# Dot attention on one Trainium2 core: one-hots built ahead of the sums over features, queries gathered one group ahead

## The reference, cut to what matters

```python
def _L2_gnn_ref(embeds, qW, kW, vW, rows, cols):      # rows = src, cols = dst
    q = (embeds[rows] @ qW).reshape(e, HEADS, dh)     # HEADS = 4, dh = 24
    k = (embeds[cols] @ kW).reshape(e, HEADS, dh)
    v = (embeds[cols] @ vW).reshape(e, HEADS, dh)
    scores = jnp.clip(jnp.einsum('ehd,ehd->eh', q, k), -10.0, 10.0)
    exp_s = jnp.exp(scores)
    norms = jax.ops.segment_sum(exp_s, rows, num_segments=nvar)[rows]
    w = exp_s / (norms + 1e-08)
    res = jax.ops.segment_sum(w[:, :, None] * v, rows, num_segments=nvar).reshape(nvar, d)
    return embeds + res
```

## Time and profile before

| | |
|---|---|
| median of 3 runs | 1662.23 us (1661.86 to 1662.38) |
| profiled execution | 1663.21 us, of which the span of the trace is 1661.0 us |
| mean granted clock of TensorE | 0.888 |
| busy over the span | PE 1248.2 us (75%), DVE 1260.6 us (76%), ACT 551.0 us (33%), POOL 379.8 us (23%) |
| dot attention, groups | from 1244.1 us (first one-hot) to 1564.8 us (last addition) |

### The profile page before, as it was taken

One profiled execution on the slowest core, in us unless ns is written; L12 is line 12 of the kernel. 1 busy time (PEld: TensorE's weight loads), 2 busy tenths in 40 slices (PEclk: granted clock), 3 DMA queues, 4 the chain that ended last, 5 costly groups with the idle time before them and its releaser, 6 DMA issues. The chain is left out here.

```text
span 1661.0 us, 45732 instructions
## 1 busy us (share of the span) xinstructions
PE 1248.2 (75%) x18543; PEld 1176.7 (71%) x18544; DVE 1260.6 (76%) x2253; ACT 551.0 (33%) x1096; POOL 379.8 (23%) x210
## 2 busy tenths in 40 slices
PE   4767777499999999999953018888747777777568
PEld 3357676399999999999952017777737667767468
DVE  7888888655555555554568989999889999999843
ACT  0047777300000000000006843333356666666411
POOL 1400000000000000000010107888814555545300
PEclk6857877599999999999986559999979999999779
DMA  0012223590000000000014745555224333332293
GB/s 10 0 54 104 108 102 105 202 419 11 3 2 3 2 2 3 2 2 2 2 62 152 259 168 199 198 195 198 82 97 160 123 138 140 121 140 101 79 343 106
DMA packets 43162, 174.41 MB, mean 105 GB/s; under 512 B 14467, under 2 KB 16044, under 8 KB 42308
## 3 DMA queue, kind: packets, MB, share of 16 engines
q1 hardware_dynamic: 42612, 170.14, 28.2%
q0 software_dynamic: 336, 1.20, 0.3%
HBM read 127.19 MB, written 44.13 MB: 103 GB/s over the span
## 5 line engine op out<-in xcount | busy, mean ns | idle before, releaser
L1151 PE MATMUL psum<-work,count 128*128 128x192 f16 x6250 | 520.2, 247 | 27.0 <-issue 20.3
L1151 PEld LDWEIGHTS psum<-work,count 128*128 128x128 f16 x6250 | 518.7, 98 | 28.5 <-issue 20.8
L1090 DVE SCALAR_TENSOR_TENSOR work<-psum,small,work 128x96 f32<-128x96 f32 x250 | 79.4, 317 | 230.1 <-PE psum L1151 230.1
L1752 PE MATMUL psum<-count 128*128 128x100 f16 (+1 forms) x1875 | 188.9, 208 | 79.1 <-DVE count L1849 61.1
L1752 PEld LDWEIGHTS psum<-count 128*128 128x128 f16 x1875 | 163.1, 98 | 96.6 <-DVE count L1849 56.1
L1484 PE MATMUL psum<-count 128*128 128x98 f16 x625 | 113.2, 209 | 134.1 <-DVE count L1531 97.8
L1817 POOL TENSOR_TENSOR count<-count 128x1000 bf16<-128x1000 f32 (+1 forms) x75 | 166.8, 2224 | 159.6 <-ACT count L1801 159.6
L928 ACT ACTIVATE work<-work 128x1248 f32<-128x1248 f32 (+1 forms) x6 | 7.2, 1203 | 567.8 <-DVE work L911 567.8
L1753 PE MATMUL psum<-count 128*128 128x100 f16 (+1 forms) x1875 | 187.9, 207 | 0.0
L1523 POOL TENSOR_TENSOR count<-count 128x970 bf16<-128x970 f32 (+1 forms) x75 | 166.7, 2236 | 91.2 <-ACT count L1516 91.2
L1753 PEld LDWEIGHTS psum<-count 128*128 128x128 f16 x1875 | 166.2, 98 | 0.0
(11 more groups left out here) (286 smaller groups left out, 2691.4 us busy)
## 6 DMA issues: line engine op xcount, KB each, us to landing
count<-bucket_rows_by_dst SPq DMA_DIRECT2D x50, 800.0 KB, 4.3
count<-bucket_rows_by_src SPq DMA_DIRECT2D x50, 800.0 KB, 4.3
count_f<-count SPq DMA_DIRECT2D x5, 4000.0 KB, 31.1
count<-count_turned SPq DMA_DIRECT2D x25, 800.0 KB, 6.2
count<-count_f SPq DMA_DIRECT2D x17, 800.0 KB, 4.3
count_turned<-x SPq DMA_DIRECT2D x25, 416.0 KB, 2.4
count_turned<-x SPq DMA_DIRECT2D x25, 384.0 KB, 2.3
work<-count_f SPq DMA_DIRECT2D x8, 800.0 KB, 4.3
```

The lines of the kernel that those rows point to most:

```text
L1151: last = nc.tensor.matmul(bank[i % BANKS], count16[:, j, i * P:(i + 1) * P], y[par][:, j, :], start=(j == 0), stop=(j == TILES - 1))
L1752: nc.tensor.matmul(slot(b, i, width), hot[:, t0 + i, :], high[:, of, at:at + width], start=True, stop=False, skip_group_check=True)
```

## The change

Two orders are changed; no instruction is added or taken away, and no buffer.

```diff
+                def gather_queries(j):
+                    s, t0, n = groups[j]
+                    if t0 == 0:
+                        pe.wait_ge(S["node_hot"], 2 * s + 1)
+                    after(pe, S["q_copied"], j)
+                    gather(0, D, node_hot[SRC][s % 2], t0, n, lambda t: s, 0).then_inc(S["q_done"], 1)
+
                 for j in range(G + 3):
+                    if j == 0:
+                        gather_queries(0)
+                    if j + 1 < G:
+                        gather_queries(j + 1)
                     if j < G:
                         s, t0, n = groups[j]
-                        if t0 == 0:
-                            pe.wait_ge(S["node_hot"], 2 * s + 1)
-                        after(pe, S["q_copied"], j)
-                        gather(0, D, node_hot[SRC][s % 2], t0, n, lambda t: s, 0).then_inc(S["q_done"], 1)
                         if t0 == 0:
                             pe.wait_ge(S["node_hot"], 2 * s + 2)
                         after(pe, S["multiplied"], j)
...
                     if j < G:
-                        n = groups[j][2]
-                        dve.wait_ge(S["multiplied"], j + 1)
-                        nc.vector.tensor_reduce(score[j % 2][:, 0:n * HEADS], product[:, 0:n * D].rearrange("p (i j) -> p i j", j=DH), AX.X, ALU.add).then_inc(S["reduced"], 1)
+                        s, t0, n = groups[j]
                         if s + 1 < TILES:
                             if t0 == 0:
                                 spot_nodes(SRC, s + 1)
@@
                                 spot_nodes(DST, s + 1)
                             else:
                                 spot_edges(s + 1)
+                        dve.wait_ge(S["multiplied"], j + 1)
+                        nc.vector.tensor_reduce(score[j % 2][:, 0:n * HEADS], product[:, 0:n * D].rearrange("p (i j) -> p i j", j=DH), AX.X, ALU.add).then_inc(S["reduced"], 1)
                         if t0 == GROUP and s >= 2:
                             add(s - 2)
```

## The result

The changed kernel takes 1680.24 us (median of 4 runs, 1675.30 to 1680.63), the kernel before 1662.31 us (median of 4, 1661.86 to 1665.99): a ratio of 1.0096, 95% interval 1.0072 to 1.0120. It is slower by 17.9 us, where 20 were forecast.

What follows compares the result with a forecast made beforehand. DVE, busy without a gap, was taken as the bound. The terms -14.0 + 10.1 + 12.8 + 2.9 = +11.8 us, plus 8 for clock falls, gave +20 and 1682 us on the median of 1662.23; range 1670 to 1691.

Steps and rivals of the forecast that it cites:

- What bounds: In the changed stage DVE is the bound, busy 303.17 of 303.30 us; any wait of DVE lengthens the stage.
- Part 1: Source one-hot moves ahead of POOL's start and takes 0.96 instead of 1.57 us, in 23 tiles: 14.0 us gained.
- Part 2: M directly behind R waits for it on the single product buffer, 0.21 us each in groups A and C: 10.1 us lost.
- Part 3: In group B, V waits for ACT's passes, 0.52 us in 22 tiles and 0.69 in tiles 0 and 1: 12.8 us lost.
- Part 4: At the stage's start, first keys wait behind group 1's queries and ACT's copy, delaying the first M: 2.9 us lost.
- Part 5: PE's idle time gathers into one piece, its clock may fall and M come late: 12 tiles at 0.7, 8 us lost.
- (a): Rival: PE's clock stays at 1.00 in the stage, +11.8, 1674 us; chance 0.27.
- (b): Rival: DVE's waits are hidden and only Part 1 and Part 4 remain, 1651 us; chance 0.05.
- (c): Rival: M's own wait for R costs nothing, 1680 us, or 1672 without the clock; chance 0.07.
- (d): Rival: source one-hots are still blocked by POOL's instruction under the edge one-hot, 14 us more than (a), 1688; chance 0.04.
- (e): Rival: PE's clock falls in every tile, 1696 us; chance 0.04.
- (f): Rival: whole kernel is a wash within 0.2% (3.3 us); chance 0.03.

Runs made afterwards that it cites:

- DVE's order alone: Kernel before with only DVE's order changed (each one-hot ahead of R), PE's order kept: 1673.9 us, ratio 1.0066.
- the kernel with more matmuls: Changed kernel plus 24 unread matmuls of 96 columns on PE in each tile, in PE's idle piece: 1676.3 us, ratio 1.0081 to the kernel before.
- PE's order alone: Kernel before with only PE's order changed (queries gathered a group ahead), DVE's order kept: 1665.7 us, ratio 1.0019.
- source one-hot behind the next M: Kernel before with the source one-hot moved to group B, between M and V, one product buffer: 1654.6 us, ratio 0.9943.

## Why the prediction was right, point by point

- **What bounds:** right. DVE was full, and each new wait of it lengthened the stage.
- **Part 1** (14.0 us gained): right. All node one-hots of the changed kernel take 1.04 to 1.05 us, and the kernel that removes only the block, with a second product buffer against M's wait, gained 14.3 in the stage. The Trainium skill (SBUF — State Buffer, "SBUF: two separate sides") has the port pair of VectorE and GpSimd as an exclusive lock, which whoever starts first holds for the whole instruction. The rows agree, 1.66 us behind POOL and 1.04 ahead of it, but for POOL's last 0.2 us: 0.24 us of overlap cost only 0.05.
- **Part 2** (0.21 a pair): right, with 1.28 from R10 to M10 where 1.27 was taken. The Trainium skill (VectorE: DVE Perf Modes, "The DRAIN you can't avoid") has the semaphore cost nothing extra, by a measurement on tensor_copy; here the wait costs 0.21 us, and the measurement of this case decides. The same section adds that a next instruction which isn't held starts earlier, and with this the rows agree: without the wait M starts 0.08 us ahead of R's end. But the 10.1 us of Part 2 are not a term that can be taken away by itself: with the wait gone, ACT's passes hold V at nearly the same time, and of 10 us only 2.4 come back.
- **Part 3** (0.52 in group B): right. 9.2 us over 24 waits is 0.38 each, as in the last tile of before, and R to V is 2.32 us where 2.31 was taken.
- Parts 1 to 3 sum up to +8.9; DVE's order alone gave +9.05 (its first V, at 8.63 us from the stage's beginning, is 0.2 us earlier than before, so the order itself cost some 9.2).
- **Part 4** (2.9): right in size, with 2.8 at the first M. The 0.15 us to react in its sum, and in the start of PE's turn in Part 5, stand in no row: PE starts 0.06 us after the end of what it waited for, as 1377.68 + 1.15 to 1378.89 shows. That keys would be late a second time if the first loss were mended was not seen.
- **Part 5** (8 us, bounds 0 and 22): right in its mechanism, mis-sized by a factor of two. The idle pieces were forecast as 2.1, 1.6 and 0.4 us and are 1.97, 1.42 and 0.42. 12 falls were taken, and 13 came. The 12 were a guess (half of the tiles), so that they came near is luck in part, though the other three traces of kernels with such a piece have 12, 12 and 14. The price of a fall was not 0.7 us but 0.3 on average: 9 late M of 0.2 to 0.7 us, 4.1 us in sum, and 4.2 by subtraction (16.0 - 9.05 - 2.8). What a fall costs is set by when it begins after PE's long idle piece:

| idle piece ends, us | clock falls after it, us | next M late by, us |
|---|---|---|
| 1327.12 | 0.1 | 0.67 |
| 1340.64 | 0.2 | 0.56 |
| 1524.69 | 0.5 | 0.32 |
| 1381.21 | 0.6 | 0.20 |
| 1275.19 | 0.8 | 0 |
| 1394.26 | 1.2 | 0 |

  These are six of the 13. All 13 falls begin 0.1 to 1.2 us after such a piece, one piece of 1.96 to 2.41 us stands in each of 24 tiles, and four falls came so late in the turn that the keys were ready in spite of them. The price had been set near the worst case of 0.9, which is itself 0.8 (1.03 + 2 x 1.60 + 0.2 is 4.43, and not 4.5, against 3.61).
- **The rivals:** (a), the clock stays, is all but the kernel with more matmuls, at 1676.3 us where 1674 was worked out. (b), hidden waits, fell with the 9.2 us of V's waits. (c) fell with the 1.28 from R to M and (d) with one-hots of 1.05 us at most. (e), a fall in every tile, fell with 13 falls in 24 tiles, and (f), no change, with the interval of 1.0072 to 1.0120.

The terms add up to 19.8 us and the span grew by 17.5. Of the difference Part 5 makes 3.8 us, against 1.5 us of the span that lie outside the stage and weren't forecast. So the total is nearer than its largest term: two errors partly cancel.

## What to carry to other kernels

On an engine that is full, what lies between a result handed to another engine and its use is not idle filler but cover. Before moving it, add up the other engine's way there and back, here 1.17 us behind R, and see what is left between. A block between two engines can often be had out of the way by placing the blocked instruction where the other is known to be idle and cover is to spare: one one-hot moved behind the next M, and a second buffer, gained 0.8% where the order with all three one-hots moved, and the queries ahead, lost 1.0%. An instruction that waits for the one directly ahead on its own engine pays 0.2 us here, but whether a second buffer gives that back depends on what else holds the next one.

## What the runs showed of the hardware

- A clock fall needs no long pause: TensorE idle for 1.96 to 2.41 us once in each 13 us was enough to bring 13 falls to 0.50 in a stage that is busy three quarters of the time, while pieces of 1.24 us (DVE's order alone) brought none. Between the two, 1.49 us once in a tile (PE's order alone) was followed by 3 falls, and 1.42 us (the kernel with more matmuls) and 1.36 (source one-hot behind the next M) by none. 24 idle-time matmuls a tile, whose results nobody reads, left 1 fall where there were 13, with a stage that is 3.3 us shorter (one trace of each kernel).
- Tiles with the same order had a fall or not (clock 1.00 behind the piece of 1.97 us at 1301.15, and 0.50 from 1341). The falls come in series: in the changed kernel six stand in a row, each 13.65 or 13.66 us after the last, while a tile takes 12.98, and they move from 0.1 us behind the idle piece at the first of the six to 1.2 at the last; then come three tiles without one. The changed kernel's runs range over 5 us; that this is the number of falls is likely but wasn't shown, as other stages vary too.
- The block between DVE and POOL ends about 0.2 us before the end that the trace gives for POOL's instruction: 0.81 us of overlap cost 0.61, 0.24 cost 0.05. Whether the block ends early or the end in the trace is late, these rows can't tell.
